# A ring of score tiles in which two heads take turns: eight tiles of the second head are summed between the first head's, and its pixels are loaded and normalised earlier

## The reference

```python
def _L1_conv_ref(x, w_out, b_out):
    N, D, H, W = x.shape
    patches = extract_patches(x)                       # 5 x 5 shifted copies, zero padded
    p = patches.reshape(N, NHEADS, hdim, K2, H, W)     # 8 heads of 8 channels, K2 = 25
    q = x.reshape(N, NHEADS, hdim, 1, H, W)
    scores = (p * q).sum(axis=2, keepdims=True)
    att = jax.nn.softmax(scores, axis=3)
    out = (p * att).sum(axis=3).reshape(N, D, H, W)
    return jnp.einsum('ndhw,od->nohw', out, w_out) + b_out[None, :, None, None]

x = x + _L0_conv_ref(_gn(x), ...)
x = x + _L1_conv_ref(_gn(x), L1_conv_w_out, L1_conv_b_out)
```

## Time and profile before

| | us |
|---|---|
| median of 3 runs | 1668.08 |
| lowest, highest | 1666.13, 1669.68 |
| the profiled execution, its own time | 1669.27 |
| its span, first to last instruction | 1667.5 |
| DVE busy | 1402.4 (84%) |
| PE busy | 1365.2 (82%) |
| POOL busy | 1138.1 (68%) |
| ACT busy | 991.9 (59%) |

### The profile page before, as it was taken

How to read it: one execution, slowest core, us unless ns; L and a number is a source line. 1 busy time by engine, 2 the same in 40 slices (tenths; PEclk the granted TensorE clock), 3 DMA queues, 4 the chain that set the end, 5 groups by cost and what they waited for, 6 DMA issues and landing times.

```text
span 1667.5 us, 62887 instructions
## 1 busy us (share of the span) xinstructions
PE 1365.2 (82%) x26281; PEld 755.7 (45%) x26281; DVE 1402.4 (84%) x1964; ACT 991.9 (59%) x1861; POOL 1138.1 (68%) x875
## 2 busy tenths in 40 slices
PE   4889999999999999646978879798796977877664
PEld 3667777777777777412322323233232322323332
DVE  4977777777777777789999999999999998994833
ACT  3667777777777777455647567474675745562200
POOL 5445555555555555306799999999999999974700
PEclk9989999999999999876999999999999998987977
DMA  8902021202033211152024233232522323235089
GB/s 325 335 16 59 19 59 23 58 19 58 19 96 35 60 28 51 45 132 54 18 54 114 55 92 83 53 83 55 127 55 60 78 46 73 55 148 172 22 332 388
DMA packets 106870, 152.35 MB, mean 91 GB/s; under 512 B 71362, under 2 KB 83650, under 8 KB 100034
## 3 DMA queue, kind: packets, MB, share of 16 engines
q1 hardware_dynamic: 106690, 149.67, 30.9%
HBM read 77.99 MB, written 65.20 MB: 86 GB/s over the span
## 4 chain that ended last, share of the span: by engine, by line
PE 42%; POOL 21%; issue 13%; DVE 11%; ACT 9%; SPq 1%; DMA 1%; POOLq 0%; ACTq 0%; DVEq 0%
POOL arena L802 14%; PE PS L1489 8%; PE PS L1324 6%; PE PS L1350 6%; PE PS L1333 5%; POOL arena L813 5%; PE PS L1301 3%; PE PS L1433 3%; PE PS L1512 3%; PE PS L1293 2%; ACT arena L991 2%; PE PS L1464 2%; DVE arena L1197 2%; POOL arena L768 2%; DVE arena L1110 2%
## 5 line engine op out<-in xcount | busy, mean ns | idle before, releaser
L1223 DVE TENSOR_TENSOR arena<-arena,PS 128x1568 f32<-128x1568 f32 x334 | 585.1, 1779 | 20.0 <-PE PS L1489 10.7
L802 POOL TENSOR_TENSOR arena<-arena 128x1568 f32<-128x1568 f32 x168 | 516.8, 3113 | 88.8 <-PE PS L1433 68.5
L768 POOL TENSOR_TENSOR arena<-arena,consts 128x196 f32<-128x196 f32 x512 | 294.4, 610 | 301.8 <-ACT arena L852 301.8
L1489 PE MATMUL PS<-arena,consts 32*32 32x392 f32 x12800 | 400.8, 515 | 74.6 <-DVE arena L1223 21.0
L1000 ACT ACTIVATE PS<-arena 128x392 f32<-128x392 f32 x334 | 166.3, 501 | 255.1 <-DVE arena L1223 253.8
L1433 PE MATMUL PS<-arena,consts 128*32 128x392 f32 x1664 | 199.8, 552 | 85.7 <-POOL arena L802 45.5
L1489 PEld LDWEIGHTS PS<-arena,consts 32*32 32x32 f32 x12800 | 147.5, 104 | 244.9 <-issue 108.0
L877 ACT ACTIVATE arena<-PS 128x452 f32<-128x452 f32 x256 | 141.2, 552 | 144.0 <-PE PS L1333 140.6
L1350 PE MATMUL PS<-arena 128*64 128x34 f32 x4096 | 196.5, 228 | 34.9 <-POOL arena L768 21.6
L813 POOL TENSOR_TENSOR arena<-arena 128x1568 f32<-128x1568 f32 x66 | 202.1, 3074 | 31.0 <-ACT arena L940 22.4
L1350 PEld LDWEIGHTS PS<-arena 128*64 128x64 f32 x4096 | 154.9, 138 | 92.0 <-issue 32.1
(11 more groups left out here) (110 smaller groups left out, 1781.3 us busy)
## 6 DMA issues: line engine op xcount, KB each, us to landing
arena<-x_wide_dram SPq DMA_DIRECT2D x32, 660.0 KB, 8.1
arena<-x_wide_dram SPq DMA_DIRECT2D x256, 67.5 KB, 2.0
x_wide_dram<-arena SPq DMA_DIRECT2D x12, 1125.0 KB
arena<-in_x_dram SPq DMA_DIRECT2D x8, 1568.0 KB, 14.9
x_wide_dram<-arena SPq DMA_DIRECT2D x64, 196.0 KB, 4.3
x_dram<-arena SPq DMA_DIRECT2D x8, 1568.0 KB, 7.5
attn_dram<-arena SPq DMA_DIRECT2D x256, 49.0 KB, 3.0
arena<-x_dram SPq DMA_DIRECT2D x8, 1568.0 KB, 19.1
```

The lines of the kernel that those rows point to most:

```text
L768: i = nc.gpsimd.tensor_tensor(k_bd[k][:, r], keys.unsqueeze(1).to_broadcast([P, HEADS_T, S]), head_mask.unsqueeze(2).to_broadcast([P, HEAD ...
L802: nc.gpsimd.tensor_tensor(tile, x_part, by, ALU.mult).then_inc(pool_tile, 1)
L1223: nc.vector.tensor_tensor(by_channel(v_tiles[n % V_RING]), shifted_values(half, k), over_channels(PS[:, 2 + n % W_BANKS, 0:PIX]), ALU.mult ...
L1489: mm = nc.tensor.matmul(PS[dst, 4 + i, 0:PIX], ident[src, src], tile[src, c * PIX:(c + 1) * PIX], start=done == 0, stop=done == NK - 1)
```

## The change

The ring takes four pairs of score tiles of head 1 (shifts t = 0 to 3, made by GpSimd) between those of head 0: one pair before each of head 0's shifts 4, 6, 8 and 10. The waits of TensorE, ScalarE and VectorE on the count of copied maps follow the new order (`PAIR_AT`), and the planner does too. VectorE's and GpSimd's own orders are the same as before. The late pixels of head 1 are issued right behind those of head 0; the store of the last image pair, which stood between them with a wait, now stands behind both. The planner may put the normalising of head 1's pixels earlier (8.0 for 32.0).

```diff
-RING_ORDER = [step for step in VECTOR_ORDER if step[0] == "score"] + [step for step in TILE_ORDER if step[0] != "scale"]
+VECTOR_SCORES = [step for step in VECTOR_ORDER if step[0] == "score"]
+SECOND_HEAD_AFTER = [4, 6, 8, 10]
+
+
+def ring_order():
+
+    order, later = [], [step for step in TILE_ORDER if step[0] != "scale"]
+    for t in range(S_TILES):
+        if t in SECOND_HEAD_AFTER:
+            order += later[:2]
+            later = later[2:]
+        order += VECTOR_SCORES[2 * t:2 * t + 2]
+    return order + later
+
+
+RING_ORDER = ring_order()
+PAIR_AT = {pair: n for n, pair in enumerate(step[1:3] for step in RING_ORDER if step[0] == "score" and step[3] == 0)}
+PAIRS = sorted(PAIR_AT, key=PAIR_AT.get)
+VECTOR_AT = {step: n for n, step in enumerate(VECTOR_SCORES)}
...
-    LOADING, FIRST_LOADS = 40.0, {("s", 0): 0.0, ("s", 1): 32.0, ("v", 0): 48.0}
+    LOADING, FIRST_LOADS = 40.0, {("s", 0): 0.0, ("s", 1): 8.0, ("v", 0): 48.0}
...
-            before = ("copy", j, t - 1) if t else ("copy", j - 1, S_TILES - 1) if j else None
+            before = ("copy",) + PAIRS[PAIR_AT[j, t] - 1] if PAIR_AT[j, t] else None
...
                     for g in GROUP_ORDER[EARLY:]:
                         load_for_scores(j, a, g, xs_loaded)
-                if j == 0:
-                    store_x1(BP - 1)
-                    for a in range(2):
-                        sp.wait_ge(xs_loaded[s_buf(0, a)], 16 * EARLY * CH)
+            store_x1(BP - 1)
             sp.wait_ge(x1_stats, UNITS)
...
-                if a == 0 and (j or t):
-                    pe.wait_ge(sc_copied, j * S_TILES + t)
+                if a == 0 and PAIR_AT[j, t]:
+                    pe.wait_ge(sc_copied, PAIR_AT[j, t])
```

More of the change, by code:

```diff
@@ L199, in merge_orders @@
             after = [freed, ("pixels", "s", j, step[3], pieces_of("s") - 1)]
-            if n < 2 * S_TILES:
+            if j == 0:
                 add("dve", step, 0.15 + 1.04e-3 * columns, after)
@@ L505, in await_ring_tile @@
         def await_ring_tile(eng, step):
-            n = RING_AT[step]
-            if n < 2 * S_TILES:
-                eng.wait_ge(dve_score, n + 1)
+            if step in VECTOR_AT:
+                eng.wait_ge(dve_score, VECTOR_AT[step] + 1)
             elif step in SQUARE_AT:
@@ L982, in seed_max @@
             def seed_max(j):
-                act.wait_ge(sc_copied, j * S_TILES + MAX_MAPS[0][0] + 1)
+                act.wait_ge(sc_copied, PAIR_AT[j, MAX_MAPS[0][0]] + 1)
                 if j:
@@ L1200, in max_step @@
                 unit, slot = MAX_MAPS[m + 1]
-                dve.wait_ge(sc_copied, j * S_TILES + unit + 1)
+                dve.wait_ge(sc_copied, PAIR_AT[j, unit] + 1)
                 if m:
```

## The result

| | before | changed |
|---|---|---|
| median | 1668.88 us, 4 runs (1666.13 to 1674.37) | 1699.93 us, 4 runs (1698.06 to 1705.02) |
| ratio | | 1.0194, 95% interval 1.0169 to 1.0218 |
| profiled execution, span | 1669.27 us, 1667.5 us | 1699.54 us, 1697.8 us |
| VectorE's first score product | 716.38 | 722.16 |
| head 0's subtraction | 779.74 | 803.18 |

The changed kernel is slower by 31 us at the median and by 30.3 in the span; 13.2 were forecast. The spans differ by +5.78 (the start), +17.66 (the rest of head 0's scores), +6.24 (head 0's values), -0.34 (heads 1 to 6) and +0.96 (the tail).

A forecast was written before the change was run, and what follows sets the result against it. VectorE bounds head 0's scores while GpSimd is free; afterwards both are full. Start +4.8, held products +18.9 and waits given back -10.5 sum to +13.2, so 1681.3 us; 8 in 10 from 1672 to 1692.

The forecast's parts named there:

- The later start: Head 0's scores: VectorE's first product waits for the store, now behind 16 more transfers; +4.8 us.
- GpSimd's tiles among VectorE's: Head 0's scores: GpSimd's eight products and VectorE's products take turns and hold each other; +18.9 us.
- the walk: Tile-by-tile count through the ring in head 0's scores: 20.5 us held, less 2.9 saved at the end, 17.6.
- the 1.3 that was taken: Head 0's scores: VectorE's waits for ring places at the slow clock, half of 2 to 3 us.
- What it gives back: Heads 1 to 6: GpSimd's lead removes part of VectorE's 15.4 us of waits; -10.5 us, between 0 and -15.4.
- a sign of being wrong: The prediction called itself wrong if VectorE's waits in heads 1 to 6 stay above 10 us.
- 4.7 lasts about six heads: Steady heads: GpSimd's carried lead of at most 4.7 us shrinks only by its 0.7 us of extra work a head.
- Rival 1: Lead gives nothing back, since TensorE's stream, not GpSimd, sets VectorE's waits; +23.7, 1691.8 us, chance 0.17.
- VectorE did not wait in head 0: Head 0's values: none of VectorE's product waits lay in this head before the change.
- The tail: From head 7's subtraction to the end: left as it was at 181.65 us; wrong if not 182 long.

The follow-up runs named there:

- The kernel with the store first: Changed kernel with the store of the last image pair back between head 0's and head 1's late pixels, without the wait: 1696.93 us, ratio 1.0176.
- The kernel with written tiles: Changed kernel with GpSimd's eight early tiles each written by two fills instead of multiplied: 1686.77 us in one execution.
- GpSimd light in every head: Changed kernel with GpSimd's score products from head 2 on multiplying two of four groups: 1686.87 us in one execution.
- the kernel with a lead there: Changed kernel with GpSimd's products of head 2's scores alone multiplying two of four groups: 1707.16 us in one execution.

## Why the prediction was wrong

**The later start** was right: +4.8 was forecast, with the store as the wait, and +5.78 came. The kernel with the store first shows it alone.

**GpSimd's tiles among VectorE's** was right in its mechanism, and by luck in its sum: head 0's subtraction was forecast at 803 and began at 803.18; the term was +18.9 and measured 17.66. Its parts were off and cancel. The five held pairs take 35.1 us for 17.5, that is +17.7, less 4.5 for the two products at the end that were held before: 13.2 for the 17.6 of the walk. The waits for ring places are 0.87 + 0.95 + 2.29 = 4.1 for the 1.3 that was taken. The kernel with written tiles shows that the turns with GpSimd are the cause.

**What it gives back** is the step that failed: -10.5 was forecast, and VectorE's waits grew by 6.8 (22.2 for 15.4). In heads 1 to 6 they stayed at 16.1 us, above the 10 that the prediction had named as a sign of being wrong. Three things in it have to be kept apart.

The cause of the waits was right in part. With GpSimd light in every head they fall to 3.5 us, so they need its lateness. But with half the matmuls of TensorE's value sums left out heads 1 to 6 become as short (594.4 and 595.5 us for 593.7), and on before GpSimd's waits at the ring, 9.9 us, are gone. So GpSimd is late because its own work nearly fills a head, and because it waits for TensorE. The prediction worked with the first, and allowed for TensorE only by taking a bit over half of the waits that name it. How the 15.4 us divide between the two stays open, since each run is one execution.

What was wrong is that "4.7 lasts about six heads". It was gone by head 2. The working got GpSimd's lead through the scaling in head 1 (28.3 - 4.7 = 23.6 us behind the subtraction; measured 24.1, with a wait of 9.17 for the scaling), and head 1 did become shorter, 98.67 us for 100.11. But then it let the lead run on at the difference of the two engines' busy times. It left out the ring: a GpSimd that is early must wait until TensorE has summed the tile four places before, and TensorE takes tiles in its planned order, between VectorE's. GpSimd lost 0.57 + 4.42 us so in head 1, 4.94 in head 2 of the kernel with a lead there, and from the next head on the lag is that of the kernel before, about 29 us. The kernel before could have told it: its lag was 28.7, 28.3 and then 28.9 us in every head to head 6, where 0.7 us a head would have made it grow, and GpSimd waited at the ring in each head from head 2 on. Rival 1 gave the right sum for these heads (nothing given back). Its mechanism, TensorE's stream and not GpSimd, has a part in what the runs showed, but not alone.

Head 0's +6.24 was in no case. "VectorE did not wait in head 0" was carried over from before. But GpSimd's first value came 12.5 us earlier against the subtraction, and more tiles, its own and VectorE's, stand in TensorE's order ahead of the last total, in a stretch where TensorE stood still neither before nor after. The growth goes with the lead: 1.1 us with no pair, 3.6 with one, 6.2 to 9.8 in the executions with four pairs, four value tiles and whole sums. How it divides among TensorE's order, the chain through ScalarE's copies and the clock around the subtraction (0.53 of full from 799.0 to 818.4 in the changed kernel, 0.70 from 775.56 to 794.0 before) stays open; taking the first away turned the wait into others, and shorter sums left 4.1 us of it.

The tail was taken as 182 and was 182.61. In all, 5.8 + 17.7 + 6.2 - 0.3 + 1.0 = 30.4 us were measured (30.3 before rounding), where the forecast had 4.8 + 18.9 - 10.5.

## What to carry to other kernels

An engine that is freed early in one stage can lose its lead at the next buffer that is full. So before a lead is carried over stages, look for the ring it writes to, for who frees its places, and for waits there in the kernel before. A lag that is the same in every stage, as the 29 us here, is a sign that waits of one engine or the other set it, and not the difference of two busy times. And an idle engine is no free engine: before work is put beside a full one, look in the trace for the two running at once, and price them from those rows. When tiles go earlier, follow them into the consumer's list as well and see what falls behind them there.

## What the runs showed of the hardware

A GpSimd fill of 128 x 1568 took 1.41 us beside VectorE's products and left them at 3.49 a pair, where GpSimd's product made a pair 5.57 to 8.73. Halving the matmuls of a value sum that share TensorE's array (8 for 16, each 32 x 32) shortened one that stands alone from 0.95 only to 0.89 us, and three in a row from 2.81 to 2.20; halving their columns shortened one to 0.62. With the halved columns the granted clock of heads 1 to 6 was 0.82 to 0.90. With the halved matmuls it was 0.91 to 0.98, as it was with whole sums (0.92 to 0.98).
